# Attention of a fused layer on one core: scores of two blocks in one TensorE burst, their banks shared with the transposed probabilities, and one group's projections spread over the first turns

## What is computed

```
q, k, v = x_in @ wq.T, x_in @ wk.T, x_in @ wv.T          # 4 heads of 64
mask    = (j <= i) & (j > i - 128)
logits  = where(mask, q k^T / sqrt(64), -1e30)
out     = softmax(logits) @ v ;  out_swa = out @ wo.T
```

## Time and profile before

| | us |
|---|---|
| median of three runs | 2393.5 |
| lowest and highest run | 2392.09, 6023.82 |
| the profiled execution | 2394.46 |
| its span | 2392.7 |
| mean granted TensorE clock | 0.995 |

### The profile page before, as it was taken

The page is one execution under the profiler, slowest core; times in us unless marked ns, Lnnn a source line. Parts: engine busy times, 40 slices in busy tenths (PEclk is TensorE's granted clock), DMA queues, the critical chain, the costliest instruction groups (busy, mean ns, idle before and its releaser), DMA issues. The chain is left out here.

```text
span 2392.7 us, 39965 instructions
## 1 busy us (share of the span) xinstructions
PE 2339.6 (98%) x14822; PEld 2077.4 (87%) x14822; DVE 1690.5 (71%) x3666; ACT 1604.1 (67%) x2443; POOL 1402.5 (59%) x1000
## 2 busy tenths in 40 slices
PE   7999999899999999999999999999999999999998
PEld 6888888788888888888888978777777789999998
DVE  6777776666666666666666676777777857777776
ACT  4787888757777777777777656666676645554453
POOL 2666666657677766667667734666666553343433
PEclk9999999999999999999999999999999999999999
DMA  4222221442323222322233222333222165555551
GB/s 129 79 84 80 88 73 63 177 154 62 71 66 71 68 62 62 67 62 63 67 67 69 84 91 87 102 102 100 90 78 77 31 150 154 137 147 145 149 141 58
DMA packets 295395, 221.74 MB, mean 93 GB/s; under 512 B 189283, under 2 KB 262024, under 8 KB 295073
## 3 DMA queue, kind: packets, MB, share of 16 engines
q1 hardware_dynamic: 281376, 188.74, 29.1%
q0 software_dynamic: 13824, 30.44, 4.3%
HBM read 113.30 MB, written 72.12 MB: 77 GB/s over the span
## 5 line engine op out<-in xcount | busy, mean ns | idle before, releaser
L2737 ACT ACTIVATE e_hf<-e_ps_z,e_b 128x640 f32<-128x640 f32 x128 | 101.8, 796 | 213.6 <-PE e_ps_z L105 192.9
L2464 POOL TENSOR_TENSOR m_hl<-m_hf,m_hh 128x512 fp32r<-128x512 f32 x112 | 157.6, 1413 | 101.9 <-ACT m_hh L2067 100.5
L2864 POOL DMA_INDIRECT out<-e_ys,slot_token x80 | 83.3, 1041 | 214.2 <-DVE e_ys L2816 208.7
L105 PE MATMUL e_ps_y<-r_w_h,e_hl 128*128 128x256 f32 x640 | 180.4, 282 | 0.0
L105 PE MATMUL e_ps_y<-r_w_l,e_hh 128*128 128x256 f32 x640 | 178.9, 280 | 0.0
L105 PE MATMUL e_ps_y<-r_w_h,e_hh 128*128 128x256 f32 x640 | 178.7, 279 | 0.0
L1650 POOL TENSOR_TENSOR halves_l<-hT_full,halves_h 128x512 fp32r<-128x512 f32 x120 | 153.7, 1303 | 38.3 <-ACT halves_h L1308 38.3
L914 POOL DMA_INDIRECT xbuf_d<-xn,scatter_rows x128 | 148.5, 1160 | 41.8 <-issue 38.6
L771 POOL TENSOR_TENSOR prob<-prob,softmax_small 128x1024 f32<-128x1024 f32 x65 | 123.2, 1896 | 72.0 <-DVE softmax_small L689 72.0
L105 PE MATMUL e_ps_z<-slotsT_h,w_l 128*128 128x320 f32 x512 | 158.5, 310 | 1.8 <-ACT e_hf L2737 1.1
L105 PE MATMUL e_ps_z<-slotsT_l,w_h 128*128 128x320 f32 x512 | 158.2, 309 | 0.0
(11 more groups left out here) (359 smaller groups left out, 9036.1 us busy)
## 6 DMA issues: line engine op xcount, KB each, us to landing
shared_xT<-xT_d SPq DMA_DIRECT2D x64, 256.0 KB, 3.6
new_w1T<-in_W SPq DMA_DIRECT2D x16, 1024.0 KB
new_w2T<-in_W SPq DMA_DIRECT2D x16, 1024.0 KB
xbuf_d<-new_w1T SPq DMA_DIRECT2D x16, 650.0 KB
shared_x<-in_x SPq DMA_DIRECT2D x16, 512.0 KB, 4.2
xn_d<-xn SPq DMA_DIRECT2D x32, 256.0 KB, 2.5
xT_d<-shared_xT SPq DMA_DIRECT2D x32, 256.0 KB, 2.6
oT_d<-shared_oT SPq DMA_DIRECT2D x32, 256.0 KB, 2.6
```

What stands on the lines that cost most here:

```text
L105: i = e.matmul(out, a, b, start=first and not onto and n == 0, stop=last and n == len(terms) - 1, skip_group_check=onto)
L2464: e.tensor_tensor(hl[:, t, 0:N], hf[(HC * C + t) % NZ][:, 0:N], hh[:, t, 0:N], ALU.subtract).then_inc(*h_low(C, t))
L2737: e.activation(hf[(HC * i + t) % NHF][:].rearrange("p (s n) -> p s n", s=2), ps_z[t % 2][:, :, 0:HALF], ACTF.Relu, bias=b1[:, i % E, t:t + ...
L2864: e.indirect_dma_start(io["out"], bass.IndirectOffsetOnAxis(ap=token[i % 2][:, b:b + 1], axis=0), ys[:, b], None, bounds_check=NT - 1, oob ...
```

## The change

**Banks.** `ps_scores` and `ps_probT` become two sets of two banks, `ps_scores0` and `ps_scores1`. Block g has its scores in set g % 2, and later its transposed probabilities in the same set. The four banks in use are the same in number.

**Order on PE.** In an even turn PE makes the scores of blocks `a` and `a + 1` one behind the other, in an odd turn none. The transposes of block g now wait until the maxima of block g + 2, which has its scores in the same set, have been taken, and until the rest of block g - 2 has been made; the scores of block g wait for the maxima of g - 2 and the rest of g - 4.

**Order on ACT.** `soft(a)` moves from behind `round_pt(a - 2)` to the start of the turn, ahead of the early projection steps.

**Order on DVE.** The maxima of an even block are made at the end of the odd turn before, ahead of that turn's late projection steps; those of an odd block in the even turn before, behind `invert` and ahead of the early steps.

**Opening.** The q, k and v projections of group 1 leave `opening()` and become late steps of turns -1, 0 and 1, two in each. They are the same instructions.

```diff
 def steps_at(a):
...
     G, j = a // GRP + 2, a % GRP
+    second = parts(1, 2 * a + 4) + parts(1, 2 * a + 5) if a < 2 else []
     if a < 0 or G >= NGRP:
-        return [], []
-    return parts(G, 2 * j) + (parts(G, 1) if j == 0 else []), parts(G, 2 * j + 1) if j else []
+        return [], second
+    return parts(G, 2 * j) + (parts(G, 1) if j == 0 else []), second + (parts(G, 2 * j + 1) if j else [])
...
 def output_at(a):
...
         for n in range(2, 8):
-            out += parts(G, n)
+            out += parts(G, n) if G != 1 else []
             if G == MEM and n == 3:
...
-        ps_s = ps("ps_scores", [P, 2, 2, 2 * P])
-        ps_pt = ps("ps_probT", [P, 2, HEADS, P])
+        ps_sets = [ps(f"ps_scores{i}", [P, 2, 2, 2 * P]) for i in range(2)]
         ps_av = ps("ps_av", [P, KC, 2 * P])
...
         def bank(*u):
...
+        def scores_of(g):
+            return ps_sets[g % 2]
+
+        def probT_of(g):
+            return ps_sets[g % 2][:].rearrange("p b c (h q) -> p b (c h) q", q=P)
+
         def last_bank(c2):
...
-            return ps_av[:, 0] if c2 == 0 else ps_s[:, 1, 0]
+            return ps_av[:, 0] if c2 == 0 else ps_sets[0][:, 1, 0]
...
         def freed(*u):
...
                 pe.wait_ge(*qk_low.at(0 if G == MEM else G, 3))
-                pe.wait_ge(*top_made.at(g - 1))
+                pe.wait_ge(*top_made.at(g - 2))
+                pe.wait_ge(*pt_low.at(g - 4))
+                ps_s = scores_of(g)
                 for c2 in range(2):
...
             def transpose_p(g):
-                p = pr[g % NPR]
+                p, ps_pt = pr[g % NPR], probT_of(g)
                 pe.wait_ge(*prob_made.at(g))
-                pe.wait_ge(*pt_low.at(g - 1))
+                pe.wait_ge(*top_made.at(g + 2))
+                pe.wait_ge(*pt_low.at(g - 2))
                 for kb in range(2):
...
                 pe.wait_ge(*av_full.at(last - 1))
-                pe.wait_ge(*top_made.at(last))
+                pe.wait_ge(*pt_low.at(last - 1))
                 for kb in range(2):
...
             def keep_busy(n):
-                pe.wait_ge(*top_made.at(last))
+                pe.wait_ge(*pt_low.at(last - 1))
                 ones = w["wq"][0]
                 for _ in range(n):
-                    e.matmul(ps_s[:, 0].rearrange("p a b -> p (a b)"), ones[:, 0, 0:P], ones[:].rearrange("p k d -> p (k d)"),
+                    e.matmul(ps_sets[0][:, 0].rearrange("p a b -> p (a b)"), ones[:, 0, 0:P], ones[:].rearrange("p k d -> p (k d)"),
                              start=True, stop=True)
...
             for a in TURNS:
                 early, late = steps_at(a)
-                if a in turns:
+                if a == MEM_BLOCK:
                     scores(a)
+                elif a % 2 == 0 and a in turns:
+                    scores(a)
+                    scores(a + 1)
                 for kind, *key in early:
...
             def round_pt(g):
...
                 act.wait_ge(*av_done.at(g - 2))
+                ps_pt = probT_of(g)
                 if g == last:
...
                     return
-                e.activation(pth[g % 2][:], ps_pt[:], ACTF.Copy).then_inc(*pt_high(g))
+                e.activation(pth[g % 2][:], ps_pt, ACTF.Copy).then_inc(*pt_high(g))
...
             def soft(g):
...
             for a in TURNS:
                 early, late = steps_at(a)
+                if a in turns:
+                    soft(a)
                 for kind, *key in early:
...
                     round_pt(a - 2)
-                if a in turns:
-                    soft(a)
                 if a - 3 in turns and a - 3 < last:
...
                     i = e.tensor_tensor_reduce(
-                        out=p[:, h], in0=ps_s[:, h % 2, h // 2], in1=masks[:, mask], scale=1.0, scalar=-3.0e38,
+                        out=p[:, h], in0=scores_of(g)[:, h % 2, h // 2], in1=masks[:, mask], scale=1.0, scalar=-3.0e38,
                         op0=ALU.add, op1=ALU.max, accum_out=sm[:, 0, h:h + 1])
...
             def rest_pt(g):
+                ps_pt = probT_of(g)
                 if g == last:
...
                 dve.wait_ge(*pt_high.at(g))
-                e.tensor_tensor(ptl[g % 2][:], ps_pt[:], pth[g % 2][:], ALU.subtract).then_inc(*pt_low(g))
+                e.tensor_tensor(ptl[g % 2][:], ps_pt, pth[g % 2][:], ALU.subtract).then_inc(*pt_low(g))
...
             def rest_w2T(k):
...
             for a in TURNS:
...
                 early, late = steps_at(a)
-                if a in turns:
+                if a == MEM_BLOCK:
                     maxima(a)
...
                     invert(a - 1)
+                if a % 2 == 0 and a + 1 in turns:
+                    maxima(a + 1)
                 for kind, *key in early:
...
                     rest_pt(a - 2)
-                for kind, *key in late:
-                    do[kind](*key)
+                if a % 2 == 0:
+                    for kind, *key in late:
+                        do[kind](*key)
                 if 0 <= a and G < NGRP and j == 0:
...
                     norm_apply(G, j - 1)
+                if a % 2 and a + 1 in turns:
+                    maxima(a + 1)
+                if a % 2:
+                    for kind, *key in late:
+                        do[kind](*key)
                 if a in w2T_turns and a - 2 < last:
```

## The result

The changed kernel takes 2456.72 us (median of six runs, 2455.65 to 2458.45) against 2393.57 for the kernel before on the same chip: ratio 1.0265, 95% interval 1.0254 to 1.0276. It is slower by 63 us, where 2445 was forecast in a range of 2425 to 2467. One of the six runs of the kernel before took 6023.82 us and is left out of the ratio. The profiled execution took 2455.78 us, its span is 2454.0 against 2392.7.

The account below looks back on a forecast made before the run. PE alone was taken to set the pace. Twelve groups +38.8, opening 0 and tail +4 gave +43; with +8 for the clock, 2394.5 became 2445.5, as a median 2445 us, range 2425 to 2467.

Parts of the forecast that it names:

- Step 1: First turn of a group: PE's second row transposes wait for rest of v, behind block a's maxima: 1.22 us.
- Step 2: Next turn's first projection on PE waits for POOL's rest of rows, behind DVE's later maxima and casts: 2.34 us.
- Step 3: Transposes of the next block on PE wait for POOL, which normalises behind the rest of the rows: 0.47 us.
- Merges: Two score bursts issued together on PE save 0.40 us each, two in a group: 0.80 us a group.
- Rival (e): Merges give nothing back, since DVE's 1.58 us a block stands in every turn: 2455 us, chance 0.05.
- Opening: Blocks before 8: 9.6 us given back, against two first turns of 4.03 and a bank wait: taken as 0.
- Tail: Turns 56 on: merges give 1.6 us, each of eight turns can meet a 1.2 us wait: +4 taken.
- Clock: Clock falls in first turns after 4.55 us without full-array matmuls other than transposes; four falls, about 2 us each: +8.
- Rival (b): Clock falls in every first turn and takes longer to rise: 2461 to 2480 us, chance 0.15.
- (a): Stalls come as worked out and the clock holds: 2437 us, chance 0.27.
- (c): The bank and buffer waits are covered, so merges and opening gain: 2374 us, 0.8% faster, chance 0.06.
- (d): First wait as told, but the first projection's wait in the next turn is shorter: 2409 to 2430 us, chance 0.12.

Follow-up runs that it names:

- the mended kernel: Changed kernel with late and early steps ahead of maxima on DVE and row copies ahead of exponentials on ACT: 2410.18 us; with a further reordering 2408.05 us.
- the fillers: Changed kernel with eight or three idle 128x512 matmuls per group ahead of the first projection of each second turn: 2445.17 and 2444.25 us.

## Why the prediction was right

**What bounds.** Right. TensorE had no slack in the groups of before, and every wait put on it appeared in full.

**Step 1, 1.22 us.** Right: the transposes start at 3.34 instead of 3.35. The trace shows 1.06, as its idle time starts at the modelled end of the matmul ahead; taking it away shortened a group by 1.14.

**Step 2, 2.34 us.** Right in size (2.31) and in its chain: held up by `transpose_p` are the maxima, then the casts, then GpSimd, then TensorE. Counted from the burst at 157.57, all of the chain runs some 0.2 late: the maxima start at 5.02 instead of 4.79, the casts at 6.60 instead of 6.37, the projection at 9.92 instead of 9.72; TensorE's own work in between is through 0.1 later as well.

**Step 3, 0.47 us.** Right within 0.11: the last projection matmul starts at 168.75 and is through 0.23 later, the transposes start at 169.34, so 0.36 us lie between. The trace names 0.19 of it as a wait.

**Merges, -0.80 a group.** The double burst takes what it should (1.62), and parting the bursts of the changed kernel costs the 1.4 us a group that the saving and the moved burst add up to. But that is a sum of two effects, and the saving is no property of the merge: in the mended kernel, where VectorE's read-outs end the third turn's wait, the saving is zero or below. Rival (e) was rejected for this kernel rightly, as its groups would take 29.6 us and those without a fall took 28.94. The Trainium skill, TensorEngine Tiling (Array Packing), section Performance Considerations (PSUM Bottleneck), says that tiling speeds up TensorE but not the emptying of PSUM; in the mended kernel the runs agree with it (2404.21 single, 2408.05 merged).

**Groups, +38.8.** Measured +40.4.

**What was costed at nothing.** ScalarE was named as the next limit once step 2 gets shorter, with 0.6 us to spare. Shortening step 2 on VectorE alone gave 0.2 of the 1.27 us taken off the wait; with step 1 and ScalarE's order mended as well the group fell from 28.74 to 26.58. The trace names ScalarE, with 1.95 us for the rows in the first turn, as expected, and 1.95 for q in the third, which the prediction did not look at; the two orders were not tried apart, so how much of the 2.16 is ScalarE's is not shown.

**Opening, 0.** Mis-sized: +2.0, outside the -1.5 to +0.5 given. The part that was mis-sized is what the spread gives back: 8.0 were booked, for two waits and the whole of the half clock, and on its own it brings block 8 forward by 5.4. The clock then stays up, but smaller waits of 0.3 to 0.6 us stand where the two of 1.9 were. The cost set against it fits: 2.0 + 5.4 + 1.6 for the merges is 9.0, a fall of the clock in it, and 8.1 to 10.1 were booked.

**Tail, +4.** Measured +5.7, inside -1.6 to +8.2. The waits are not those of step 1, which had lent the tail its size: three bursts of scores stand for the rest of the probabilities, and five times the transposes stand for maxima. Up to 1.7 of it is one fall of the clock (the window 490 to 500 us has 0.83).

```profile
PE ps_scores L433 <- DVE probT_l L712: 3.7, 3, 1.7
PE ps_scores L444 <- DVE softmax_small L692: 2.8, 5, 0.9
```

**Clock, four falls of 2 us, +8.** The term has the right size by two errors: nine falls of 1.3 us, 11.8. And its mechanism is wrong. I placed the falls in the first turn, behind the stretch without full-array matmuls. They begin at the end of step 2's wait or up to 1.5 us behind it, in the next turn's projections. With that stretch broken up they stay (2457.94); with the wait filled, wholly or in part, they go (2445.17 and 2444.25). I had looked at the one fall of the kernel before and taken for its cause what preceded it first, the scores and transposes, when a wait of 1.88 us stood in it as well.

Rival (b) is nearest in frequency, nine of its twelve, and has the price too high: 12 x 2 at the least, against 11.8 in all. The Trainium skill, TensorE: Matmul & The Clock Gate, section A second HAM failure mode: psum-queue depth-cycling, tells of small idle gaps that make the clock go up and down; the trace agrees that it goes down and up once in nine of the twelve groups, and the fillers show that the falls need the gap. Rivals (a), (c) and (d) fell: the clock did not hold, no wait was covered, step 2 was not shorter.

The profiled execution came out 10.3 us above the 2445.5 of the sum: 1.6 in the groups' waits (4% of them), 3.8 in the clock, 2.0, 1.7 and 1.3 in opening, tail and rest. The waits, which follow from a fixed order of instructions, could be added up; what I chose within a band was too low each time. The prediction also took two per cent for what a measurement of this kernel can tell from no change. The intervals here are 0.1 to 0.2% on either side, which is why a gain of 4.2 us can be told.

## What to carry to other kernels

When two blocks of work are issued together on the engine that sets the pace, write down what the engines behind it do first: here two merges saved 0.80 us a group by the prediction's rows, and waits took 4.2 and the clock 1.0. Look at the orders of those engines before the banks: mending three of them gave back 46.5 of 63 us. And try the parts of a change apart: the smallest, a respread opening, gains 4.2 us alone, and it is the only version here that beat the kernel before.

## What the runs showed of the hardware

The granted clock fell from 2.4 to 1.2 GHz behind waits of 2.23 to 2.65 us, once a group, in nine groups of twelve, each time for about 3.4 us. It did not come during the wait: in two groups it came with its end, in the others 0.5 to 1.5 us behind it, when TensorE was at work again. Equal waits did not act alike: 2.29 us at 167.49 without a fall, 2.30 at 256.72 with one. With the wait of 1.06 ahead of it removed, falls came in four groups instead of nine. With waits of 1.6 us in that place none came in twelve groups. Yet in the changed kernel's tail a fall began at 489.9, 2.0 us behind the end of a wait of 1.59; ahead of block 8 of the version with eight idle matmuls one followed a wait of 1.82; and with single bursts one followed a wait of 1.77. So the length of one wait does not decide it, and what decides between two equal waits stays open. Idle matmuls in a wait that is there anyway gave back 11 to 12 us of 63, without changing a single dependency.
